# One queue for the modulation weights, and another order of TensorE's work in windowed attention

## What is computed

```python
mod = (silu(c) @ wmod).reshape(4, 6, 1, 1024)       # sa, ca, ga, sb, cb, gb
h = layernorm(x) * (1 + ca) + sa
x = x + ga * attn_block(h)     # LN, QKV, windowed attention, projection, LN, MLP 1024-4096-1024
h = layernorm(x) * (1 + cb) + sb
x = x + gb * moe(h)            # 8 experts of 512, the two best gated, all computed densely

# windowed attention: 16 heads of 64, windows of 128 tokens
sim  = einsum('bnid,bnjd->bnij', q * 0.125, kk)     # kk: the window, the one before, the one after
attn = softmax(where(valid, sim, min))
out  = einsum('bnij,bnjd->bnid', attn, vv)
```

## Time and profile before

| | us |
|---|---|
| median of 2 runs | 2896.76 (2894.13 to 2899.39) |
| the profiled execution | 2891.51 |
| its span on the slowest core, core 6 | 2889.9 |
| spans of the eight cores | 2879.4 to 2889.9 |
| modulation weights, until the last cast | about 96 |
| attention | about 825 to 1322 |

### The profile page before, as it was taken

One profiled execution on the slowest core, in us unless ns is written; L12 is line 12 of the kernel. 1 busy time (PEld: TensorE's weight loads), 2 busy tenths in 40 slices (PEclk: granted clock), 3 DMA queues, 4 the chain that ended last, 5 costly groups with the idle time before them and its releaser, 6 DMA issues.

```text
span 2889.9 us, 32310 instructions; the slowest of 8 cores (2879.4 to 2889.9 us)
## 1 busy us (share of the span) xinstructions
PE 1772.3 (61%) x10437; PEld 930.2 (32%) x10437; DVE 811.1 (28%) x1708; ACT 778.5 (27%) x1694; POOL 74.6 (3%) x140
## 2 busy tenths in 40 slices
PE   0320355535776776674356888888711179999999
PEld 0100111212334444442223555555400134444443
DVE  2224332232114444433222111111133311111111
ACT  0002222222234444441002222222233322222222
POOL 0000000000000000000120000000011100000000
PEclk9855677767866566565667888988855589999999
DMA  8242111111233323222662111110166511111110
GB/s 263 89 132 94 59 49 61 59 58 66 88 110 103 96 88 103 81 67 96 195 198 102 44 45 45 44 37 30 35 207 210 204 41 37 37 37 37 37 37 33
DMA packets 109425, 249.37 MB, mean 86 GB/s; under 512 B 30505, under 2 KB 44977, under 8 KB 107214
## 3 DMA queue, kind: packets, MB, share of 16 engines
q1 hardware_dynamic: 69936, 140.84, 15.8%
q10 hardware_dynamic: 27938, 60.33, 5.4%
q0 software_dynamic: 11392, 46.15, 4.9%
HBM read 186.95 MB, written 60.32 MB: 86 GB/s over the span
## 4 chain that ended last, share of the span: by engine, by line
PE 53%; DVE 16%; DMA 13%; ACT 8%; issue 7%; ACTq 1%; DVEq 1%; SPq 0%; PEldq 0%; POOL 0%; PEld 0%; POOLq 0%
PE bank L1664 8%; PE bank L1218 7%; PE bank L1197 7%; PE bank L1678 6%; PE bank L662 5%; DMA arena<-wfc2T 5%; PE bank L956 3%; PE bank L899 3%; DMA arena<-w_in 3%; PE bank L812 3%; DMA arena<-wmod 2%; PE bank L696 2%; DMA arena<-wqkvT 2%; PE bank L1647 1%; PE bank L924 1%
## 5 line engine op out<-in xcount | busy, mean ns | idle before, releaser
L1218 PE MATMUL bank<-arena 128*128 128x256 bf16 x2048 | 288.6, 289 | 156.2 <-DVE arena L1131 99.5
L1218 PEld LDWEIGHTS bank<-arena 128*128 128x128 bf16 x2048 | 210.5, 103 | 248.7 <-issue 168.4
L1197 PE MATMUL bank<-arena 128*128 128x512 bf16 x1024 | 274.1, 392 | 0.3 <-ACT arena L1226 0.3
L1678 PE MATMUL bank<-arena 128*128 128x512 bf16 x1024 | 244.1, 381 | 3.7 <-DMA arena<-s_h2T 3.7
L632 PE MATMUL bank<-ident_bf,arena 128*128 128x128 bf16 x144 | 18.2, 306 | 362.1 <-DVE arena L626 362.1
L1664 PE MATMUL bank<-arena 128*128 128x512 bf16 x1024 | 239.3, 379 | 0.0
L1226 ACT ACTIVATE arena<-bank,arena 128x256 bf16<-128x256 f32 x256 | 121.2, 474 | 425.8 <-PE bank L1218 425.8
L956 PE MATMUL bank<-arena 64*128 64x128 bf16 x768 | 116.2, 291 | 108.0 <-ACT arena L969 90.0
L1687 ACT ACTIVATE arena<-bank 128x512 f32<-128x512 f32 x128 | 76.4, 597 | 378.7 <-PE bank L1681 264.9
L1691 DVE TENSOR_SCALAR arena<-arena 128x512 bf16<-128x512 f32 x128 | 62.3, 486 | 375.9 <-ACT arena L1687 375.9
L969 ACT ACTIVATE arena<-bank 128x384 bf16<-128x384 f32 x256 | 124.7, 488 | 149.2 <-PE bank L956 106.2
(11 more groups left out here) (184 smaller groups left out, 2174.6 us busy)
## 6 DMA issues: line engine op xcount, KB each, us to landing
arena<-x_ext SPq DMA_DIRECT2D x34, 512.0 KB, 5.2
arena<-wfc2T POOLq DMA_DIRECT2D x64, 256.0 KB, 4.3
arena<-wfc1T SPq DMA_DIRECT2D x64, 256.0 KB, 4.5
arena<-w_in POOLq DMA_DIRECT2D x64, 256.0 KB, 3.8
arena<-s_s SPq DMA_DIRECT2D x32, 512.0 KB, 5.1
arena<-w_in SPq DMA_DIRECT2D x64, 256.0 KB, 5.2
arena<-wmod POOLq DMA_DIRECT2D x8, 1536.0 KB, 8.3
arena<-wmod SPq DMA_DIRECT2D x8, 1536.0 KB, 8.6
```

The lines of the kernel that those rows point to most:

```text
L1197: st=tT_r[mu % 2]: e.matmul(bf(b)[:, :], st[:, l * 128:(l + 1) * 128], wfc2_bf[:, mm * 1024 + nn * 512: mm * 1024 + nn * 512 + 512], start ...
L1218: e.matmul(bf(b)[:, 0:256], wfc1_bf[:, kk * DFF + mm * 128: kk * DFF + mm * 128 + 128], zt[:, kk * 256:(kk + 1) * 256], start=(kk == 0), s ...
L1678: e.matmul(bf(b)[:, :], ht[:, ts(kk, 128)], w1_bf[:, (ee * 8 + kk) * 512:(ee * 8 + kk) * 512 + 512], start=(kk == 0), stop=False))
```

## The change

It has two parts. In the first, all 16 loads of `wmod` are issued by SyncE, with one semaphore for each staging buffer. Their waits stay the same.

In the second, the work of a head in attention is emitted in another order: the transposes of the head two back, the V matmuls of the head four back, and at h = 6 the projection, come before the head's scores and no longer after its exponential and reciprocal. Two kinds of waits are left out: the one for `SEXP` before the scores from the third head on (the transposes ahead of them wait for the same value), and the one for `SPTEp` before the V matmuls, but for the last two heads of a tile.

```diff
     for k in range(8):
         for h in range(2):
             i = k * 2 + h
-            qeng = "sync" if i % 2 == 0 else "gpsimd"
-            qsem = LDmod[0] if i % 2 == 0 else LDmodG
             if i >= 2:
-                waitr(qeng, CAST0, i - 1)
-            E.op(qeng, lambda e, kk=k, hh=h, ii=i: e.dma_start(
+                waitr("sync", CAST0, i - 1)
+            E.op("sync", lambda e, kk=k, hh=h, ii=i: e.dma_start(
                 wstage[ii % 2][:, :],
                 wmod[ts(kk, 128), hh * 3072:(hh + 1) * 3072]),
-                inc=qsem.bump(16))
-            E.wait("vector", qsem, qsem.n)
+                inc=LDmod[i % 2].bump(16))
+            E.wait("vector", LDmod[i % 2], LDmod[i % 2].n)
...
-        def emit_v(idx):
+        def emit_v(idx, skip_pte=False):
...
-            waitr("tensor", SPTEp[idx % 2], idx // 2 + 1)
+            if not skip_pte:
+                waitr("tensor", SPTEp[idx % 2], idx // 2 + 1)
...
-            waitr("tensor", SEXP, idx - 1)
+            if h > 1:
+                emit_tr_copy(idx - 2)
+            if h > 3:
+                emit_v(idx - 4, skip_pte=True)
+            if h == 6 and t > 0:
+                tail_proj(t - 1)
+            if h < 2:
+                waitr("tensor", SEXP, idx - 1)
...
-            if h > 1:
-                emit_tr_copy(idx - 2)
-            if h > 3:
-                emit_v(idx - 4)
-            if h == 6 and t > 0:
-                tail_proj(t - 1)
         for fl in (HEADS - 2, HEADS - 1):
             emit_tr_copy(t * HEADS + fl)
-        for fl in (HEADS - 4, HEADS - 3, HEADS - 2, HEADS - 1):
-            emit_v(t * HEADS + fl)
+        for fl, sk in ((HEADS - 4, True), (HEADS - 3, True),
+                       (HEADS - 2, False), (HEADS - 1, False)):
+            emit_v(t * HEADS + fl, skip_pte=sk)
```

More of the change, by code:

```diff
@@ L342, in build_program @@
                                           AF.Copy), inc=MODEV.bump())
-    LDmodG = _alloc_sem("LDmodG")
-    LDmodG.base = 0
     for k in range(8):
```

## The result

The changed kernel is slower by a third of a per cent: ratio 1.0034, 95% interval 1.0021 to 1.0048, with medians of 2905.45 us for it and 2895.36 us for the kernel before. 2894 was forecast, a gain of 3; it lost 10. The measured time lies within the stated range, and the direction is wrong.

The account below looks back on a forecast made before the run. The prediction saw 53% TensorE and 13% loads on the chain, attention mostly at 1.2 GHz. Loads -9 us and the wait after the projection +6 gave -3: 2896.8 to 2894 us, range 2876 to 2914.

Parts of the forecast that it names:

- The wait that moves closer: Attention rounds: transposes wait sooner on their head's exponential, met with 0.17 or 0.10 us to spare; cost nothing, bound 19 us.
- rival A: Attention: exponential late for the transposes in each of 12 rounds of 16 tiles, 19 us slower, 2913 us; chance 0.12.
- The waits taken away are worth nothing: Attention: dropping waits before scores and V matmuls gains nothing; the exponential's was met long ago and transposes ask the same.
- After the projection: Attention at h = 6, 15 tiles: fewer matmuls done under the wait for the held-up exponential; 0.39 us each, 6 us lost.
- Start and end of a tile cancel: Attention tile: 0.1 us lost at the start waiting for head 2's exponential, 0.10 gained at the last head's transposes.
- The loads: Modulation weight loads in the first 96 us: one SyncE queue at 5.0 us a load, last cast done at 86.8, 9 us saved.
- the first load can land at 9.9: Start of the modulation loads: issued at 3.5 us plus the shortest landing seen, 6.4 us.
- B: Modulation loads: one queue runs better than two that share, 4.4 us each, 18 us saved, 2885 us; chance 0.13.
- D: Modulation loads: one queue moves only 204 GB/s, 7.7 us a load, 31 us lost, 2934 us; chance 0.04.
- C: Modulation loads: memory and not order limits them, 5.35 us a load, 4 us saved, 2899 us; chance 0.10.

Follow-up runs that it names:

- the kernel with only 25.28 us outside it: Changed kernel with the exponential's wait last and the projection emitted again behind the scores of head 6, against the kernel before: ratio 0.9976 (0.9937 to 1.0015).

## Why the prediction was wrong

**The wait that moves closer** is the step that failed. The prediction put "TensorE would go on about 0.1 later: 1.29" and concluded "It is met with 0.17 to spare, 0.10 where a copy of 0.48 on ScalarE comes first." No row of it has that 0.1; the nearest is the 0.15 of S(9), where one wait stands alone before the scores. Before the transposes two stand, and for odd heads three, with the exponential's as the first; the true figure is 0.25 and 0.36 to 0.39, so 1.43 and 1.54 to 1.57 us from the start of S, against 1.46 available. Even heads were just in time, odd heads were late: T(9) starts 0.51 after S(10), where 0.43 is the least. That is rival A in a part of the rounds, from the point that it named, and the room that the range leaves for A is why the time still lies in it. The rounds are only 0.15 us a tile of the 0.71, though; the rest is at T(0), T(2), T(6) and T(15), which wait for the exponential in any case and where the forecast used the same 0.1. The kernel shows three waits in `emit_tr_copy` (the third, for SAOE, is missing from the list of waits in front), so they could have been counted.

**The waits taken away are worth nothing**: they had been met, and the experiments agree that waits worked off ahead of time are free. The step then took waits as free everywhere, which they are only ahead of the late one.

**After the projection**, 0.39 us: 0.34 and 0.47 by the experiments. **Start and end of a tile cancel**: together with that step the order itself costs 0.24 us outside the projection once the wait stands last (25.75 against 25.51), where the sum of the steps was 0.39. Right within 0.15; the start cost nothing (6.93 us to the projection before, 6.50 with one group of scores of 0.43 fewer). The Trainium skill's rule that a change of tiling mode drains the array (TensorEngine Tiling (Array Packing), Key Properties) was no part of the loss beyond what the steps had.

**The projection itself** was taken as fixed. It is 0.23 us longer in the mean, with the clock's rise falling at another place in each tile; the kernel with only 25.28 us outside it gained nothing in the tile either. That the longer tile fell out of step with the clock is argued from these lengths and not shown apart.

**The loads**, 9 us: the term was mis-sized by 4. The loads ran as worked out: from the first cast to the last, (92.0 - 1.8 - 14.9) / 15 = 5.0 us each, and before (96.7 - 1.8 - 17.2) / 15 = 5.2. What failed is "the first load can land at 9.9": the first cast started at 14.9. On core 5 the DMA engines were 78% busy from 4 to 8 us and moved 129 GB/s, in the kernel before 286 GB/s (windows, columns as above, first the changed kernel, then the one before):

```profile
4.00:8.00 4.00, 0.00 (x0) 0.00 (x0) 0.00 (x0) 0.00 (x0) 0.00 (x0) 1.00 0.78 129
8.00:12.00 4.00, 0.00 (x0) 0.00 (x0) 0.08 (x1) 0.11 (x1) 0.00 (x0) 1.00 0.90 246
```

```profile
4.00:8.00 4.00, 0.00 (x0) 0.00 (x0) 0.00 (x0) 0.00 (x0) 0.00 (x0) 1.00 0.88 286
```

Both large loads now stand behind six small ones in SyncE's queue; before, GpSimd issued one of them at 1.58 us. That this is what keeps the first load from landing sooner was not tried alone, so the cause of these 5 us stays open. Rivals B and D are out. C forecast 4 us, and 4.7 came, but with 5.0 us a load and not the 5.35 of its sum. (The 2872 in B, for 3.7 us a load, should be about 2874.)

So -9 and +6 became -5 and +18 by the traces: 11 of the 12 us by which attention was missed are waits in the wrong order (0.71 x 15), and the rest is the projection's length, 3 us, less 2 us for the order's own steps.

## What to carry to other kernels

Of several waits ahead of an instruction, put the one that is met last at the end. The others are then worked off for nothing while the engine is still busy, and each that stands behind it adds its own time to the path. Before an order is changed so that a wait moves closer, count how many more waits stand behind it. And where a stage alternates between dense and sparse work on TensorE, judge an edit by its pieces: here the clock swallowed the 0.47 us that one edit saved in every tile, and added 0.23 to each in the changed kernel.

## What was not expected of the hardware

- A met wait behind a late one costs TensorE 0.11 us: from the row sum's end 0.15 us with none, 0.25 with one, 0.36 to 0.39 with two, 0.47 with three, 0.58 with four. From the end of VectorE's copy it is the same: 0.15 with none, 0.25 with one, 0.47 with three. Ten such waits ahead of transposes that were not held up cost 0.01 us in a stretch of 6.9 us.
- Stretches of equal work had lengths from 4.8 to 6.2 us in one run, by when the clock rose in them. Kernels with 25.3 to 25.8 us of other work in a tile had the same tile, 30.75 to 30.79; with 26.46 it was 31.95.
- Two loads in flight in one queue kept 5.0 us a load of 1.57 MB, and in two queues, one of them GpSimd's, 5.2.
